# SiLU behind FiLM in the attention part: ScalarE's own function between two table changes, in place of three ScalarE steps and a GpSimd product

## What is computed

```
xn = layernorm(x) * norm_scale + norm_bias
q, k, v = xn @ Wq + bq, xn @ Wk + bk, xn @ Wv + bv      # keys and values masked
q = softmax(q per head, over the 32 features);  k = softmax(k, over the tokens)
attn = k^T v  (per head);  y = q attn
emb_out = silu(emb) @ film_emb_W + film_emb_b;  scale, shift = split(emb_out)
h = layernorm(y) * (1.0 + scale) + shift
h = jax.nn.silu(h) @ film_out_W + film_out_b             # silu(h) = h * sigmoid(h)
return x + h
```

## Time and profile before

| quantity | value |
|---|---|
| time, median of 3 runs | 4806.68 us (4803.45 to 4808.08) |
| time of the profiled execution | 4803.31 us |
| its span, first to last instruction | 4801.3 us |
| what lies around the span (the difference) | 2.0 us |
| busy share of the span: TensorE, VectorE, GpSimd, ScalarE | 90%, 86%, 82%, 68% |
| attention part, from its table load to the end | 3619.03 us to 4801.3 us |

### The profile page before, as it was taken

The page is one execution under the profiler, slowest core; times in us unless marked ns, Lnnn a source line. Parts: engine busy times, 40 slices in busy tenths (PEclk is TensorE's granted clock), DMA queues, the critical chain, the costliest instruction groups (busy, mean ns, idle before and its releaser), DMA issues. The chain is left out here.

```text
span 4801.3 us, 74789 instructions
## 1 busy us (share of the span) xinstructions
PE 4343.3 (90%) x21344; PEld 3077.7 (64%) x21344; DVE 4110.9 (86%) x5035; ACT 3262.8 (68%) x7813; POOL 3932.5 (82%) x1828
## 2 busy tenths in 40 slices
PE   7898889988898989888889989999878999999998
PEld 4666666666666666666666666666655666666655
DVE  2999999999999999999999999999995665665664
ACT  2888788887887888788878878888762333333332
POOL 1999999999999999999999999999993333343332
PEclk9999999999999999999999999999989999999999
DMA  5111111111111111111111111111122232222321
GB/s 200 41 45 47 45 46 47 45 58 54 62 45 45 45 47 45 48 45 52 60 55 53 45 45 47 45 47 45 45 84 90 92 100 87 98 88 87 104 82 46
DMA packets 122574, 301.03 MB, mean 63 GB/s; under 512 B 15409, under 2 KB 20785, under 8 KB 121714
## 3 DMA queue, kind: packets, MB, share of 16 engines
q1 hardware_dynamic: 120610, 288.52, 17.5%
q10 hardware_dynamic: 1616, 8.39, 0.4%
HBM read 245.35 MB, written 51.51 MB: 62 GB/s over the span
## 5 line engine op out<-in xcount | busy, mean ns | idle before, releaser
L787 POOL TENSOR_TENSOR dbu<-du,bc 128x1024 f32<-128x1024 f32 x1024 | 2453.9, 2488 | 103.1 <-DMA bc<-b_scratch 94.2
L491 ACT ACTIVATE dA<-dt,c_A 128x256 f32<-128x256 f32 x4096 | 1698.6, 463 | 520.0 <-DVE hC L655 498.7
L744 DVE TENSOR_TENSOR_SCAN dA<-dA,dbu 128x512 f32<-128x512 f32 x1088 | 1288.6, 1212 | 21.8 <-ACT dA L491 18.3
L744 DVE TENSOR_TENSOR_SCAN hS<-dA,dbu 128x512 f32<-128x512 f32 x960 | 1157.5, 1212 | 108.5 <-ACT dA L491 50.2
L798 POOL TENSOR_TENSOR hS<-hS,bc 128x1024 f32<-128x1024 f32 x480 | 1193.4, 2486 | 15.9 <-DVE hS L744 15.9
L325 PE MATMUL Y<-c_ident,hC 128*128 128x128 f32 x4352 | 584.2, 278 | 159.4 <-DVE hC L655 159.2
L325 PEld LDWEIGHTS Y<-c_ident,hC 128*128 128x128 f32 x4352 | 500.4, 142 | 296.4 <-DVE hC L655 216.4
L655 DVE TENSOR_TENSOR hC<-dA,bc 128x1024 f32<-128x1024 f32 x544 | 653.1, 1201 | 0.0
L325 PE MATMUL Y<-c_ident,hS 128*128 128x128 f32 x3840 | 510.1, 277 | 4.7 <-POOL hS L798 4.7
L390 PE MATMUL side<-xin,c_conv_w 128*128 128x256 f32 x2048 | 500.7, 379 | 0.7 <-DVE zs L676 0.7
L366 PE MATMUL side<-sh_weights,sh_tile 128*128 128x512 f32 x1024 | 501.1, 608 | 0.0
(11 more groups left out here) (132 smaller groups left out, 5460.2 us busy)
## 6 DMA issues: line engine op xcount, KB each, us to landing
bc<-b_scratch SPq DMA_DIRECT2D x256, 512.0 KB, 3.7
sh_tile<-in_x SPq DMA_DIRECT2D x64, 512.0 KB, 6.1
o_scratch<-oS SPq DMA_DIRECT2D x64, 256.0 KB, 2.0
sh_tile<-o_scratch SPq DMA_DIRECT2D x32, 512.0 KB, 4.7
sh_tile<-gate_scratch SPq DMA_DIRECT2D x32, 512.0 KB, 5.7
x_scratch<-p_x_in SPq DMA_DIRECT2D x32, 512.0 KB, 3.2
p_xr<-x_scratch SPq DMA_DIRECT2D x32, 512.0 KB, 6.8
out<-p_xr SPq DMA_DIRECT2D x32, 512.0 KB, 2.9
```

The costliest lines, as they stand in the source:

```text
L491: last = act.activation(dA[:, q % A_RING, e, :], dt[j % 2][:, e, :], ACT.Exp, scale=C["A"][:, 2 * j + e, n:n + 1])
L744: dve.tensor_tensor_scan(out.rearrange("p e t -> p (e t)"), dA[:, q % A_RING, :, :].rearrange("p e t -> p (e t)"), dbu[(q // 2) % B_RING][ ...
L787: gps.tensor_tensor(dbu[p % B_RING][:, :, :, :], du[j % 2][:, :, :].unsqueeze(1).broadcast_to([P, 2, 2, GT]), bc[:, 0, n:n + 2, :].unsquee ...
```

## The change

The three ScalarE passes become one pass with the function `Silu`, which writes `hF` itself. The tile `ht`, two semaphores and GpSimd's product go away. In every step with Cc the table `silu_and_others` is loaded ahead of the two SiLU instructions, ahead of their wait for `hp`, and `natural_log_exp_and_others` is loaded again behind them. SiLU now waits for the earlier film product of the same buffer, as GpSimd's product did.

```diff
     hp = sb("hp", [P, GB, D])
-    ht = sb("ht", [P, GB, D])
     hF = sb("hF", [P, GB, D])
...
             if B:
                 exp_queries(g, 1)
             if Cc:
+                act.preload_act_table_set("silu_and_others")
                 for b in range(GB):
                     wait(act, s["hp_done"], c * 2 + (b + 1))
-                    wait(act, s["hF_done"], c * 2 + (b - 1))
-                    act.activation(ht[:, b, :], hp[:, b, :], ACT.Exp, scale=-1.0).then_inc(s["h_step"], 1)
-                for b in range(GB):
-                    wait(act, s["h_step"], c * 4 + (b + 1))
-                    act.activation(ht[:, b, :], ht[:, b, :], ACT.Ln, bias=1.0).then_inc(s["h_step"], 1)
-                for b in range(GB):
-                    wait(act, s["h_step"], c * 4 + (b + 3))
-                    act.activation(ht[:, b, :], ht[:, b, :], ACT.Exp, scale=-1.0).then_inc(s["hsig_done"], 1)
+                    wait(act, f["F"], c * 2 + (b - 1))
+                    act.activation(hF[:, b, :], hp[:, b, :], ACT.Silu).then_inc(s["hF_done"], 1)
+                act.preload_act_table_set("natural_log_exp_and_others")
...
                 for b in range(GB):
                     gps.tensor_tensor(xr[:, b, :], xr[:, b, :], bo[:, :], ALU.add).then_inc(s["xb_done"], 1)
-                for b in range(GB):
-                    wait(gps, s["hsig_done"], c * 2 + (b + 1))
-                    wait(gps, f["F"], c * 2 + (b - 1))
-                    gps.tensor_tensor(hF[:, b, :], hp[:, b, :], ht[:, b, :], ALU.mult).then_inc(s["hF_done"], 1)
```

More of the change, by code:

```diff
@@ L878, in attention @@
              "q_emptied qmax_done qsub_done qe_done qsum_r rq_done kT_done qF_done at_done y_emptied bn_b st_b lnv_b rstd_b "
-             "yhat_done hp_done h_step hsig_done hF_done xb_done f_done").split()
+             "yhat_done hp_done  hF_done xb_done f_done").split()
     s = {n: sem("p3_" + n) for n in names}
```

## The result

The changed kernel takes 4769.8 us (median of 4 runs, 4763.1 to 4774.0); the kernel before takes 4807.4 us beside it. The ratio is 0.992, 95% interval 0.9903 to 0.9937. 4774 us had been forecast.

The account below looks back on a forecast made before the run. TensorE, full in the attention part, was taken as the bound, losing 0.76 us per step to waits. Gains of 22.4 + 0.7 + 9.7 = 32.8 us, from a 4806.7 us median, gave 4774 us; range 4768 to 4790.

Parts of the forecast that it names:

- its two waits: TensorE's waits for qF (at values(0)) and hF (at the film product), 0.38 us lost per step at each.
- undisturbed step: Attention loop step in which TensorE waits for neither qF nor hF: 34.78 us, against 35.54 on average before.
- waits that were put at nothing: Places where delay was to cost nothing, such as the residual's additions in the steps, with 5.8 us of cover.
- x: What a table load between two activations costs beyond its 1.28 us record; bounded 0 to 1.74 us, taken as 0 to 0.2.
- further 1.38 us for a drain: Rival at the load before qF: it drains ScalarE; 4804 us, or 4807 by the skill's figure; chance 0.12.
- rival of half the gain: TensorE misses 34.78 us a step through another wait, or SiLU takes twice the exponential's time; 4785 us, chance 0.10.
- The end: Steps 31 and 32, where TensorE waits long for qF and hF: 0.7 and 9.7 us to be gained.
- 0.7 us at `qF` of step 31: Shorter ScalarE chain to qF takes 0.71 us directly off TensorE's 7.27 us wait in step 31.
- 9.7 us behind it: Gain in step 32 from earlier hF and a faster last film product; range 8.6 to 10.1 us.
- upper bound: Largest gain in step 32, 10.1 us, with the last addition starting near the end of the residual's bias additions.
- 11.4 hang on qF and 11.0 on hF: Split of the 22.4 us gain in steps 1 to 30 between TensorE's waits for qF and hF.
- Without this cover it would cost its 1.28 us once more: First load is hidden in 4.22 us of ScalarE idle time before hp; uncovered, it would cost another 1.28 us.

Follow-up runs that it names:

- e1: Kernel before with one unused table load between the last ScalarE pass and the qF copies, old table reloaded behind them; median 4834.7 us.
- e2: Changed kernel with one more, unused table load directly ahead of its second load; median 4800.7 us.
- e4: Kernel before with ScalarE's two qF copies moved ahead of the SiLU passes; median 4800.6 us.
- e3: Kernel before with GpSimd's product that makes hF moved ahead of the bias addition to the residual; median 4784.4 us.
- e5: Kernel before with both orders changed: GpSimd's product ahead of the residual's addition, qF copies ahead of the three passes; median 4774.2 us.
- e8: Changed kernel with the first table load moved behind the wait for hp, out of ScalarE's idle time; median 4781.7 us.
- e6: Changed kernel with the qF copies moved ahead of SiLU, between the first table load and the SiLU instructions; median 4761.1 us.
- e7: Changed kernel timed again, unaltered, against the kernel before; median 4766.4 us, ratio 0.9926.
- e9: Kernel before with SyncE's DMA queue loading the residual first in each step, compute engines untouched; median 4791.5 us.

## Why the prediction was right

- The bound was read rightly. TensorE's start-to-start distances at its two waits, and nothing else in the step, carried the gain. The undisturbed step was forecast with 34.78 us and measured with 34.77. From step 1 to step 30, 1030.7 us became 1008.4, that is -22.2 us for a forecast of -22.0. The waits that were put at nothing, for the residual in the steps above all, stayed at nothing.
- The price of the load was the open number, x from 0 to 1.74. In the changed kernel SiLU and load together take 1.94 us to `qF`, for a sum of 1.91; so x is 0.03. The Trainium skill (ScalarE: Activation LUTs, What ACT_TABLE_LOAD costs) is right with about 1.28 us for the load; its further 1.38 us for a drain are not in any of these traces, neither behind one load (`e1`: 1.40 us for everything) nor behind two (`e2`).
- SiLU cost the 0.63 us that was taken, and the rival of half the gain, a new wait behind the two old ones, did not come up.
- The end was undersized by about one us. The forecast had 0.7 us at `qF` of step 31 and 9.7 us behind it, with bounds of 8.6 and 10.1. From the attention output of step 31 to the film product of step 32 the time went from 23.04 to 14.06 us, and from there to the last addition from 8.82 to 7.17. That is 10.6 us, 0.5 beyond the upper bound. The last film product ran as forecast, 7.13 us for 7.1. What the sum left out is that everything in step 32 moves up too: step 31's film product took 7.80 us instead of 8.21, so the last `hp`, `hF` and the store that frees `xr` came 0.4 us sooner, and the residual landed 0.65 us sooner. The upper bound had held the residual's landing fixed.
- Against that, step 31's `qF` gave 0.6 us and not 0.7, and step 30 gave 0.3 and not 0.4. With 22.2 and 10.6 these are 33.7 of the 33.9 us. How much the end gives is in part chance: the 8.78 us of the last film product before are the shortest of the four traces with that long a wait, the others have 9.53 to 10.01.
- The split "11.4 hang on qF and 11.0 on hF" is wrong as two separate gains, though the sum is right. Both waits stand ahead of the same film product, and the end of the second was pinned by a DMA. `qF` alone gave 1.3 us (`e4`), `hF` alone 15.4 with its part at the end (`e3`), both 27.4 (`e5`). In the changed kernel both fall together, so the error did not show in its time.
- "Without this cover it would cost its 1.28 us once more" was oversized: 13.7 us instead of some 28, because of the wait for the second half of `hp` and the slack of `qF` (`e8`).
- Of the 40.0 us between the two profiled executions 6.1 are scatter of the Mamba part, which had no place in the sum. The medians, 37.6 us apart in the first comparison and 34.7 in the second, hold some of it too. So the mechanism is judged better by the attention part, 32.8 us forecast and 33.9 and 33.5 measured, than by 4774 against 4769.8.

## What to carry to other kernels

Where one engine is full, count its waits from start to start against a step that has none of them; small waits were worth 22 us here. The profile's list of waits has them mainly on the weight loads (15.6 us for `qF` and 36.6 us for `hF`; on the matmuls nothing and 12.9 us), and its sums are not the time lost. Before adding the gains of two removed waits, ask whether they end at the same instruction and what pins the later one: remove the later first. And look for what an operand stands behind in a neighbour's queue before replacing how it is computed: two changes of order, without the new function, gave 27 of the 34 us.

## What the hardware showed unexpectedly

A table load between two activations costs little more than its record of 1.28 us. In `e1` it starts 0.02 us behind the activation, the next activation starts 0.01 us behind the load, and 0.09 us go because the two neighbouring activations overlapped by that much before (the last pass ends at 4091.49, `qF` starts at 4091.40). A second load directly behind the first adds another 1.28 us (`e2`).

TensorE's granted clock at the end is worth more than the idle time ahead of it suggests, and does not follow its length. The sixteen matmuls of the last film product, from the timelines of all eleven traces:

| traces | wait ahead, us | sixteen matmuls, us |
|---|---|---|
| changed, `e2`, `e6`, `e7` | 1.22 | 7.13 each |
| `e8` | 2.56 | 8.83 |
| `e3`, `e5` | 5.39 | 8.88, 9.84 |
| `e1`, `e9`, `e4`, before | 9.57, 9.64, 9.70, 9.78 | 9.89, 10.01, 9.53, 8.78 |

The difference is the time at the lower level: the clock was 0.50 in the first 3 us of 8.78 before, and 0.50 in the first 4.55 us of 9.84 in `e5`. The same wait of 5.39 us came with 8.88 and with 9.84 us; what decides between them no run here shows.
